# Spreading the experts' gates by transfers from DRAM instead of selector matmuls, with a ring for h

## The chip, the cores and the metric

One core of one Trainium2 chip. Times are device microseconds of one execution; the time of the kernel before is the median of three runs. The profile is of one execution of the same kernel.

## The reference, cut to what matters

A block of cross attention is followed by a mixture of experts. With x (after attention and a residual) normalised to xf, 1024 tokens of 128 features, 64 experts of 64 hidden features, and the 8 best experts of each token:

```python
aff = xf @ centroids.T
_, idx = top_k(aff + expert_biases, 8)
w = sigmoid(take_along_axis(aff, idx)); w = w / (sum(w) + 1e-8)
cw = zeros((T, E)).at[arange(T)[:, None], idx].add(w)
h = silu(einsum('td,edf->etf', xf, W_up))
y = einsum('etf,efd->etd', h, W_down)
routed = einsum('etd,te->td', y, cw)
x = x + silu(xf @ Ws_up) @ Ws_down + routed
```

The kernel computes all 64 experts for all tokens and multiplies h by the gate cw, which is zero for the experts that a token did not choose.

## The kernel before, in words

The attention stage (to about 294 us) runs 32 steps of pair and batch; then x is normalised again, the gates are found, and the expert stage runs. Its work is tiled into 32 expert tiles f: two experts of 64 hidden features fill the 128 rows, and the 1024 tokens are the columns. Everything there is in transposed form, rows are hidden features.

For each tile, by engine:
- **TensorE** (from L866 on): `up(f)` is six fp32r matmuls of 512 columns, two halves of the tokens by three terms (high by high, high by low, low by high: `three`, L715 to L720, whose lines L718 to L720 carry up and down alike). `spread(f)` (L936 to L944) is two f16 matmuls that multiply a selector, a column cut of `sel16`, by `cwT16`, and leave in PSUM bank CW_BANK the gate of each row's expert for all tokens. `down(f)` (L949) is six matmuls that add into the Y banks. The loop at L989 does spread(f+2), up(f+6), down(f) for f from 0 to 15; the rest is an order written out by hand, `closing` (L197 to L206), with one spread ahead of every third half of up or down.
- **ScalarE**: `silu(f)` (L670) moves up's result from PSUM to `h`; `h_high(f)` (L675) rounds the weighted h into `h_hi`, a ring of two, once down(f-2) is done. They alternate: h_high(f), silu(f+5).
- **VectorE**: `weigh(f)` (L1336, instruction L1340) multiplies h in place by the spread gates in PSUM; `h_low(f)` (L1342, L1344) is h less h_hi. Order: weigh(f+2), h_low(f+1). The last six tiles have halves of their own, `last_hi` and `last_lo` (L1365), without a wait for down.
- **GpSimd**: `split_up(f+6)` and then `split_down(f)` (L431 to L439) cut 128 x 128 weights into a high and a low half, one cast (L425) and one subtraction (L428) each; the halves have two buffers, so split_up(f) waits for up(f-2) and split_down(f) for down(f-2). L462 to L466 do the same for the last six tiles.
- **SyncE** issues the transfers, in order (L286 to L342). It issues none in the expert stage but the output's.

`h` has room for all 32 tiles ([P, 32, 1024] in f32). Ahead of the stage, VectorE makes `combine`, the gates as tokens by experts, splits it into two f16 terms `cw16` (L1326 to L1332); TensorE transposes them in eight transposes behind up(3) (L958 to L967), VectorE copies the result to `cwT16` (L1334). The selector is built by GpSimd (`pick16`, L363 to L368, at the start of the kernel) and spread by ScalarE in two fills, `fill_selector` (L625 to L632 and L653), among the roots and normalisations of the second norm: fill 0 stands ahead of xh (L648), fill 1 ahead of `root2(3, 3)` (L654), which the second half of the expert input waits for.

The lines that set the order around the change:

```python
            with pe.Fori(0, CLOSING // 2) as i:
                for u in range(2):
                    f = i * 2 + u
                    spread(f + 2)
                    pe.wait_ge(s_silu, f + (LEAD - 1))
                    up(f + LEAD, u)
                    down(f, u)
```

Of the kernel before, what the change touches and what calls it, by code (L numbers as in the profile page):

```python
# [32 lines left out]
P = 128  # L33
# [9 lines left out]
def xattn_moe(nc, x, ctx_in, mask, g_x, b_x, g_l, b_l, wq, wkv, wout, g_o, b_o,  # L43
# [14 lines left out]
    LEAD = 6  # L58
    assert D == P and TILES == 4 and KEYS == 512 and NT == 8 and LEAD % 2 == 0

    stack = ExitStack()
    with stack:
# [4 lines left out]
        def lay(offset, specs):  # L67
# [12 lines left out]
        (ident, one16, ident16, zeros16, cols, stats, mv, rs, shift, tmp, pick16, ones, range_v, neg_max, p_bias, ln_range, p_sum, p_rinv,  # L80
         ), top = lay(base, [
            ("ident", [P, P], F32), ("one16", [P, P], F16), ("ident16", [P, P], F16), ("zeros16", [P, 512], F16),
            ("cols", [P, 4], F32), ("stats", [P, 2 * NT, 6], F32), ("mv", [P, 2 * NT, 2], F32),
            ("rs", [P, 2 * NT], F32), ("shift", [P, 2 * NT], F32), ("tmp", [P, 2, 2 * NT], F32),
            ("pick16", [P, E], F16), ("ones", [P, P], F32), ("range_v", [P, 8], F32),
# [16 lines left out]
        v_base = max(end1, end2)  # L102
# [32 lines left out]
        (h,), h_end = lay(h_base, [("h", [P, FT, T], F32)])  # L135
        over = -(-(h_end - raw_base) // (P * 4))
        assert over <= FT - LEAD and h_base + T * 4 <= v_end


        (outT,), _ = lay(h_base, [("outT", [P, T], F32)])  # L140
        (yT, y_out, last_hi, last_lo, last_wd_hi, last_wd_lo), last_end = lay(h_base, [
# [6 lines left out]
        UNDER = -(-(last_end - h_base) // (T * 4))  # L148
        assert UNDER + LEAD < LAST

        SCRATCH = 10
        (xh, xfT, hs, biased, left, gate, combine, cw16), end3 = lay(h_base + (FT - SCRATCH) * T * 4, [
            ("xh", [P, NT, P], F32), ("xfT", [P, T], F32), ("hs", [FF, T], F32),
            ("biased", [P, NT, E], F32), ("left", [P, NT, E], F32),
            ("gate", [P, NT, E], F32), ("combine", [P, NT, E], F32), ("cw16", [P, NT, 2, E], F16),
        ])
        assert SCRATCH <= FT - LEAD and end3 <= raw_base

        (sel16, h_hi, h_lo, cwT16, wd_hi, wd_lo, wu_hi, wu_lo, wsu_hi, wsu_lo, xf_hi, xf_lo), end3 = lay(step_base, [
            ("sel16", [P, E, FF], F16), ("h_hi", [P, 2, T], F32R), ("h_lo", [P, 2, T], F32R),  # L160
            ("cwT16", [P, T], F16), ("wd_hi", [P, 2, P], F32R), ("wd_lo", [P, 2, P], F32R),
# [100 lines left out]
        s_cw, s_cwt, s_cwT, s_sel = sem("s_cw"), sem("s_cwt"), sem("s_cwT"), sem("s_sel")  # L262
        s_pick = sem("s_pick")
# [4 lines left out]
        s_u, s_cwb, s_silu, s_h, s_hhi, s_hlo, s_down = (sem("s_u"), sem("s_cwb"), sem("s_silu"),  # L268
# [17 lines left out]
        def _(sp):  # L286
# [61 lines left out]
        def _(pool):  # L348

            pool.memset(ident[:, :], 0.0).then_inc(s_pool, 1)  # L350
            pool.memset(one16[:, :], 0.0).then_inc(s_pool, 1)
            pool.memset(ident16[:, :], 0.0).then_inc(s_pool, 1)
            pool.memset(zeros16[:, :], 0.0).then_inc(s_pool, 1)
            pool.memset(wkT[:, :, :, :], 0.0).then_inc(s_pool, 1)
            pool.memset(pick16[:, :], 0.0).then_inc(s_pick, 1)
            pool.memset(ones[:, :], 1.0).then_inc(s_pool, 1)
            pool.memset(ln_range[:, :], LN_RANGE16).then_inc(s_pool, 1)
            pool.wait_ge(s_pool, 3)
            for m, fill in ((ident, 1.0), (one16, 1.0), (ident16, 1.0 / RANGE16)):
                pool.affine_select(out=m[:, :], in_=m[:, :], compare_op=ALU.not_equal, fill=fill,  # L360
                                   base=0, pattern=[[-1, P]], channel_multiplier=1).then_inc(s_pool, 1)

            pool.wait_ge(s_pick, 1)  # L363
            for part in range(2):
                pool.affine_select(out=pick16[:, :], in_=pick16[:, :], compare_op=ALU.not_equal,
                                   fill=1.0 / RANGE16, base=-part * E, pattern=[[-1, E]],
                                   channel_multiplier=1).then_inc(s_pick, 1)
                pool.wait_ge(s_pick, part + 2)  # L368

# [100 lines left out]
        def _(act):  # L470
# [51 lines left out]
            act.wait_ge(s_pool, 10)  # L522
# [102 lines left out]
            def fill_selector(half):  # L625

                cut = slice(half * E // 2, (half + 1) * E // 2)
                act.activation(sel16[:, cut, :], pick16[:, cut].unsqueeze(2).broadcast_to([P, E // 2, FF]),  # L628
                               ACT.Copy).then_inc(s_sel, 1)

            act.wait_ge(s_pick, 3)
            fill_selector(0)  # L632

# [19 lines left out]
            fill_selector(1)  # L653
# [16 lines left out]
            def silu(f, u):  # L670
                act.wait_ge(s_u, f + 1)
                act.activation(h_all[:, bass.ds(f * T, T)].rearrange("p (a c) -> p a c", a=2),  # L672
                               ps[:, U_BANK + 2 * u:U_BANK + 2 * u + 2, :], ACT.Silu).then_inc(s_silu, 1)

            def h_high(f, u, guard=True):  # L675
                act.wait_ge(s_h, f + 1)
                if guard:
                    act.wait_ge(s_down, f - 1)
                act.activation(h_hi[:, u, :], h_all[:, bass.ds(f * T, T)], ACT.Copy).then_inc(s_hhi, 1)  # L679
# [15 lines left out]
            with act.Fori(1, LAST // 2 - 1) as i:  # L695
                h_high(i * 2 + 1, 1)
                silu(i * 2 + LEAD, 0)
                h_high(i * 2 + 2, 0)
                silu(i * 2 + (LEAD + 1), 1)
# [14 lines left out]
        def _(pe):  # L714
# [8 lines left out]
            pe.wait_ge(s_pool, 10)  # L723
# [212 lines left out]
            def spread(f, guard=True):  # L936

                if guard:
                    pe.wait_ge(s_h, f)
                w = sel16[:, :, :].rearrange("p e f -> p (e f)")[:, bass.ds(f * P, P)]  # L940
                for half in range(2):
                    mm = pe.matmul(ps[:, CW_BANK + half, :], w, cwT16[:, half * 512:(half + 1) * 512],  # L942
                                   start=True, stop=True)
                mm.then_inc(s_cwb, 1)  # L944

# [31 lines left out]
            spread(1)  # L977

# [53 lines left out]
        def _(dve):  # L1032
# [266 lines left out]
            def find(half):  # L1299
# [3 lines left out]
                for j in range(4 * half, 4 * half + 4):  # L1303
# [18 lines left out]
            chain(dve.tensor_scalar(w_sum[:, 0, :], w_sum[:, 0, :], COMBINE_EPS, 1.0 / RANGE16, ALU.add, ALU.mult))  # L1322
# [3 lines left out]
            chain(dve.tensor_tensor(combine[:, :, :], gate[:, :, :],  # L1326
                                    w_sum[:, 1, :].unsqueeze(2).broadcast_to([P, NT, E]), ALU.mult))
            chained()
            chain(dve.tensor_copy(cw16[:, :, 0, :], combine[:, :, :]))
            chained()  # L1330
            dve.tensor_tensor(cw16[:, :, 1, :], combine[:, :, :], cw16[:, :, 0, :], ALU.subtract)\
               .then_inc(s_cw, 1)  # L1332
            dve.wait_ge(s_cwt, 1)
            dve.tensor_copy(cwT16[:, :], ps[:, CW_BANK, :].bitcast(F16)).then_inc(s_cwT, 1)  # L1334

            def weigh(f):  # L1336
                dve.wait_ge(s_silu, f + 1)
                dve.wait_ge(s_cwb, f + 1)
                hv = h_all[:, bass.ds(f * T, T)].rearrange("p (a c) -> p a c", a=2)
                dve.tensor_tensor(hv, hv, ps[:, CW_BANK:CW_BANK + 2, :], ALU.mult).then_inc(s_h, 1)  # L1340

            def h_low(f, u):  # L1342
                dve.wait_ge(s_hhi, f + 1)
                dve.tensor_tensor(h_lo[:, u, :], h_all[:, bass.ds(f * T, T)], h_hi[:, u, :].bitcast(F32), ALU.subtract)\  # L1344
# [9 lines left out]
            with dve.Fori(0, CLOSING // 2) as i:  # L1354
                for u in range(2):
                    weigh(i * 2 + (2 + u))
                    h_low(i * 2 + (1 + u), 1 - u)
            for what, f in closing_low:
# [41 lines left out]
```

## Time and profile before

| what | before |
|---|---|
| median of three runs | 431.31 us (430.63 to 432.95) |
| the profiled execution: its time, which is its span | 431.2 us |
| TensorE busy | 359.6 us (83%) |
| VectorE busy | 278.3 us (65%) |
| ScalarE busy | 280.7 us (65%) |
| GpSimd busy | 272.8 us (63%) |
| expert stage | about 322 to 425 us |

Busy times of the engines are sums over the whole span, and stages with different limits are mixed in them; the rows below are of the expert stage and of what leads to it. In rows of a timeline the first number is the start in us, the second the duration in us, then engine, line, operation, what it writes and what it reads; in square brackets is the idle time of the engine before it and what ended that. PE is TensorE, DVE VectorE, ACT ScalarE, POOL GpSimd, SPq SyncE's queue. Under the name L425 or L428 stand the casts and subtractions for up's and down's weights alike. A matmul's recorded duration is longer than the step from one to the next, since they are pipelined.

### The profile page before, as it was taken

Reading aid. Unit: us, or ns where it says so; the run is one execution under the profiler, and the core shown is the slowest. Engines: PE = TensorE matmul, PEld = TensorE weight load, DVE = VectorE, ACT = ScalarE, POOL = GpSimd, SP = SyncE. Lnnn points to the kernel's source line nnn. Section 1 sums busy time; section 2 is a strip of 40 time slices with the busy share of each in tenths; the row PEclk is TensorE's granted clock in tenths of the full one; section 3 lists DMA queues with packets and bytes.
Section 4 is the critical chain, followed back from the end, with each engine's and each line's share of the span. In section 5 each row is a group of like instructions: output and inputs, shape, how many; then the busy total and the mean of one; then the engine's idle time right before and its main releaser. Section 6 shows DMA issues by size and latency. Waiting matters only on the chain. (4 is left out here: it accounts for less than half of the span.)

```text
span 431.2 us, 7500 instructions
## 1 busy us (share of the span) xinstructions
PE 359.6 (83%) x2225; PEld 273.1 (63%) x2225; DVE 278.3 (65%) x668; ACT 280.7 (65%) x571; POOL 272.8 (63%) x347
## 2 busy tenths in 40 slices
PE   3669789888979999889798897843489999999996
PEld 2447557666757777667676676633266777777774
DVE  2889677646564657465665555505767877777795
ACT  3777786858585687775876767630558666666671
POOL 4222045878678798877987877752314677776682
PEclk9999989999998999999999998986559999999999
DMA  7200053998997989999989899991000000000001
GB/s 237 68 0 2 0 97 58 179 172 164 167 156 147 186 164 174 177 168 174 173 148 196 151 163 181 145 215 51 0 1 1 2 0 0 0 0 0 2 0 49
DMA packets 154913, 42.76 MB, mean 99 GB/s; under 512 B 144768, under 2 KB 154496, under 8 KB 154880
## 3 DMA queue, kind: packets, MB, share of 16 engines
q1 hardware_dynamic: 154448, 40.78, 52.1%
q10 hardware_dynamic: 432, 1.57, 1.1%
q8 instruction: 16, 0.26, 0.3%
q14 instruction: 17, 0.14, 0.1%
HBM read 8.26 MB, written 0.52 MB: 20 GB/s over the span
## 5 line engine op out<-in xcount | busy, mean ns | idle before, releaser
L396 POOL TENSOR_TENSOR p<-prob,p 128x512 f16<-128x512 f32 x128 | 145.9, 1166 | 48.2 <-ACT p L567 47.2
L1160 DVE CUSTOM_DVE_ANT_0 sc<-ps,mask_add 128x512 f32<-128x512 f32 x128 | 87.8, 691 | 46.3 <-PE ps L720 25.2
L551 ACT ACTIVATE prob<-sc,p_bias 128x512 f32<-128x512 f32 x128 | 90.6, 710 | 0.1
L816 PE MATMUL ps<-pT,v 128*64 128x256 f16 x768 | 53.0, 291 | 33.0 <-DMA pT<-p 33.0
L567 ACT ACTIVATE p<-prob 128x512 f16<-128x512 f32 x64 | 40.3, 630 | 49.2 <-DMA pT<-p 48.4
L816 PEld LDWEIGHTS ps<-pT,v 128*64 128x64 f16 x768 | 44.8, 117 | 39.1 <-issue 39.0
L388 POOL CAST p<-prob 128x512 f16<-128x512 f32 x64 | 39.0, 614 | 20.7 <-DMA pT<-p 20.4
L1340 DVE TENSOR_TENSOR h<-h,ps 128x1024 f32<-128x1024 f32 (+1 forms) x32 | 39.1, 1221 | 18.6 <-PE ps L942 17.3
L718 PE MATMUL ps<-kv_hi,q_hi 128*128 128x512 f32 x128 | 50.8, 397 | 0.0
L720 PE MATMUL ps<-kv_hi,q_lo 128*128 128x512 f32 x128 | 50.0, 390 | 0.0
L719 PE MATMUL ps<-kv_lo,q_hi 128*128 128x512 f32 x128 | 49.9, 390 | 0.0
L1180 DVE TENSOR_TENSOR ao<-ps,rinv_sb 128x256 f32<-128x256 f32 x32 | 13.6, 425 | 47.7 <-PE ps L839 47.5
L672 ACT ACTIVATE h<-ps 128x1024 f32 (+1 forms) x32 | 32.7, 1027 | 17.1 <-PE ps L720 17.1
L425 POOL CAST wu_hi<-wup_s 128x128 fp32r (+1 forms) x30 | 24.6, 819 | 24.5 <-PE ps L720 24.3
L679 ACT ACTIVATE h_hi<-h 128x1024 fp32r (+1 forms) x26 | 27.6, 1061 | 13.1 <-PE ps L720 12.0
L1344 DVE TENSOR_TENSOR h_lo<-h,h_hi 128x1024 fp32r<-128x1024 f32 x26 | 32.2, 1239 | 0.0
L559 ACT ACTIVATE p_bias<-neg_max,ln_range 128x2 f32<-128x2 f32 x64 | 18.2, 285 | 18.7 <-DVE neg_max L1160 18.7
L839 PE MATMUL ps<-ao,wo_s 128*128 128x256 f32 x64 | 24.0, 459 | 6.7 <-DVE ao L1180 6.7
L718 PE MATMUL ps<-xf_hi,wu_hi 128*128 128x512 f32 x60 | 28.8, 480 | 0.0
L1194 DVE SCALAR_TENSOR_TENSOR v<-ps,range_v,v 128x512 f16<-128x512 f32 x32 | 23.1, 749 | 7.2 <-ACT v L580 7.1
L718 PEld LDWEIGHTS ps<-kv_hi,q_hi 128*128 128x128 f32 x128 | 24.0, 188 | 5.6 <-DVE neg_max L1160 0.4
L720 PEld LDWEIGHTS ps<-kv_hi,q_lo 128*128 128x128 f32 x128 | 24.0, 188 | 5.3
(194 smaller groups left out, 745.0 us busy)
## 6 DMA issues: line engine op xcount, KB each, us to landing
pT<-p SPq DMA_TRANSPOSE x128, 3.3
wup_s<-in_L_ffn_W_up SPq DMA_DIRECT2D x8, 256.0 KB, 3.6
wdn_s<-in_L_ffn_W_down SPq DMA_DIRECT2D x8, 256.0 KB, 4.6
wkv_s<-in_L_xattn_Wkv ACTq DMA_DIRECT2D x2, 512.0 KB, 6.9
x_in<-in_x SPq DMA_DIRECT2D x2, 256.0 KB, 8.0
wq_s<-in_L_xattn_Wq ACTq DMA_DIRECT2D x1, 512.0 KB, 7.6
tok<-in_ctx SPq DMA_DIRECT2D x4, 128.0 KB, 8.1
wo_s<-in_L_xattn_Wout SPq DMA_DIRECT2D x1, 512.0 KB, 5.4
```

The costliest lines, as they stand in the source:

```text
L388: pool.tensor_copy(p16[:, t, 0, :], prob[:, t, :]).then_inc(s_phi_pool, 1)
L396: pool.tensor_tensor(p16[:, t, 1, :], prob[:, t, :], p16[:, t, 0, :], ALU.subtract).then_inc(s_plo, 1)
L551: act.activation(prob[:, t, :], sc[:, t, :], ACT.Exp, bias=p_bias[:, t:t + 1], scale=-1.0, accum_out=p_sum[:, i % 2, t:t + 1]).then_inc(s_ ...
L567: act.activation(p16[:, t, 0, :], prob[:, t, :], ACT.Copy).then_inc(s_phi_act, 1)
L672: act.activation(h_all[:, bass.ds(f * T, T)].rearrange("p (a c) -> p a c", a=2), ps[:, U_BANK + 2 * u:U_BANK + 2 * u + 2, :], ACT.Silu).th ...
L718: pe.matmul(o, a_hi, b_hi, start=start, stop=False, skip_group_check=skip)
L719: pe.matmul(o, a_hi, b_lo, start=False, stop=False, skip_group_check=skip)
L720: return pe.matmul(o, a_lo, b_hi, start=False, stop=stop, skip_group_check=skip)
L816: mm = pe.matmul(ps[cut, AV_BANK, 0:S], v16[:, b * KT + j, v, pair * P + head * DH:pair * P + (head + 1) * DH], pT[:, i % 2, head, p * KT ...
L1160: return dve.tensor_tensor_reduce(sc[:, t, :], ps[:, SCORE_BANK + (i * TILES + t) % SCORE_BANKS, :], mask_add[:, i % B, :], -SCALE, -LEAST ...
L1340: dve.tensor_tensor(hv, hv, ps[:, CW_BANK:CW_BANK + 2, :], ALU.mult).then_inc(s_h, 1)
L1344: dve.tensor_tensor(h_lo[:, u, :], h_all[:, bass.ds(f * T, T)], h_hi[:, u, :].bitcast(F32), ALU.subtract)\
```

## The change

The selector, its two f16 terms and the selector matmuls go. The gates are made in f32 (`combine`, laid out as four tiles of two token halves by 64 experts), turned by four f32 transposes, copied to `cwT` (rows: token half by expert; 512 columns) and stored to a DRAM buffer `kept` of 256 KB. For each tile SyncE then issues two transfers, one for each expert, that read that expert's two rows of 512 gates and write them into all 64 rows of the tile in `spread_w`, a ring of four slots; the transfers of tile f wait until weigh(f-4) is done. `weigh` reads `spread_w`. `h` has 12 slots: silu(f) waits for h_low(f-12). What shared its memory (scratch, last_hi and so on) moves behind the ring, so that the wait of the first `last_hi` for old tiles goes. ScalarE's and VectorE's loops are written out. The order of the remaining matmuls and of `closing_low` is the same.

```diff
...
+        (spread_w, cwT, h_hi, h_lo, wd_hi, wd_lo, wu_hi, wu_lo, wsu_hi, wsu_lo, xf_hi, xf_lo), end3 = lay(step_base, [
+            ("spread_w", [P, SLOTS, T], F32), ("cwT", [P, T // 2], F32), ("h_hi", [P, 2, T], F32R), ("h_lo", [P, 2, T], F32R),
...
+        kept = nc.dram_tensor("gates_turned", [P, T // 2], F32, kind="Internal").ap()
...
+            sp.wait_ge(s_cwT, 1)
+            sp.dma_start(kept, cwT[:, :]).then_inc(s_kept, 16)
+            sp.wait_ge(s_kept, 16)
+            for f in range(FT):
+                if f >= SLOTS:
+                    sp.wait_ge(s_h, f - SLOTS + 1)
+                for part in range(2):
+                    e = 2 * f + part
+                    sp.dma_start(spread_w[part * FF:(part + 1) * FF, f % SLOTS, :].rearrange("p (a t) -> p a t", a=2),
+                                 kept.rearrange("(a e) t -> e a t", a=2)[e:e + 1, :, :].broadcast_to([FF, 2, T // 2]))\
+                        .then_inc(s_gates[f % SLOTS], 16)
...
-            act.wait_ge(s_pick, 3)
-            fill_selector(0)
-
...
-            fill_selector(1)
             root2(3, 3)
...
             def silu(f, u):
                 act.wait_ge(s_u, f + 1)
-                act.activation(h_all[:, bass.ds(f * T, T)].rearrange("p (a c) -> p a c", a=2),
+                if f >= RING:
+                    act.wait_ge(s_hlo, f - RING + 1)
+                act.activation(h[:, f % RING, :].rearrange("p (a c) -> p a c", a=2),
                                ps[:, U_BANK + 2 * u:U_BANK + 2 * u + 2, :], ACT.Silu).then_inc(s_silu, 1)
...
-                    for j in range(NT):
-                        mm = pe.transpose(t16[:, j * P:(j + 1) * P],
-                                          cw16[:, j, :, :].rearrange("p a e -> p (a e)"), one16[:, :])
+                    for j in range(NT // 2):
+                        mm = pe.transpose(ps[:, CW_BANK, j * P:(j + 1) * P],
+                                          combine[:, j, :, :].rearrange("p a e -> p (a e)"), ident[:, :])
                     mm.then_inc(s_cwt, 1)
-                if f == LEAD - 1:
-                    pe.wait_ge(s_sel, 2)
-                    pe.wait_ge(s_cwT, 1)
-                    spread(0, guard=False)
...
-            spread(1)
-
...
-                    spread(f + 2)
                     pe.wait_ge(s_silu, f + (LEAD - 1))
                     up(f + LEAD, u)
                     down(f, u)
-            for what, f, half in closing:
+            for what, f, half in halves:
...
             def weigh(f):
                 dve.wait_ge(s_silu, f + 1)
-                dve.wait_ge(s_cwb, f + 1)
-                hv = h_all[:, bass.ds(f * T, T)].rearrange("p (a c) -> p a c", a=2)
-                dve.tensor_tensor(hv, hv, ps[:, CW_BANK:CW_BANK + 2, :], ALU.mult).then_inc(s_h, 1)
+                dve.wait_ge(s_gates[f % SLOTS], 32 * (f // SLOTS + 1))
+                dve.tensor_tensor(h[:, f % RING, :], h[:, f % RING, :], spread_w[:, f % SLOTS, :], ALU.mult).then_inc(s_h, 1)
...
```

## Rows read from the trace of the kernel before

**Rows 1.** Windows: stretch, its us, busy us of PE, PEld, DVE, ACT, POOL, PEclk, DMA

```profile
340.00:380.00 40.00, 40.00 (x178) 29.99 (x177) 30.00 (x26) 26.23 (x26) 29.26 (x52) 1.00 0.00 0
```

**Rows 2.** The chain of work that ended last: start us, us, engine and line, merged

```profile
342.63 0.45 PE ps L942 x2
...
345.81 0.45 PE ps L942 x2
```

**Rows 3.** Timeline of GpSimd and VectorE over one expert tile, 354 to 358 us

```profile
353.99 1.22 DVE L1344 TENSOR_TENSOR h_lo<-h,h_hi 128x1024 fp32r<-128x1024 f32 x1
...
354.17 1.18 POOL L425 CAST wu_hi<-wup_s 128x128 fp32r x1 [0.48 <-PE ps L720]
...
355.53 0.46 POOL L428 TENSOR_TENSOR wu_lo<-wup_s,wu_hi 128x128 fp32r<-128x128 f32 x1 [0.18 <-POOL wu_hi L425]
...
355.94 0.29 POOL L425 CAST wd_hi<-wdn_s 128x128 fp32r x1
...
356.02 1.22 DVE L1340 TENSOR_TENSOR h<-h,ps 128x1024 f32 x1 [0.82 <-PE ps L942]
...
356.41 0.47 POOL L428 TENSOR_TENSOR wd_lo<-wdn_s,wd_hi 128x128 fp32r<-128x128 f32 x1 [0.18 <-POOL wd_hi L425]
...
357.16 1.22 DVE L1344 TENSOR_TENSOR h_lo<-h,h_hi 128x1024 fp32r<-128x1024 f32 x1
```

**Rows 4.** Timeline of GpSimd and VectorE in the closing part, single rows

```profile
381.86 0.46 POOL L428 TENSOR_TENSOR wd_lo<-wdn_s,wd_hi 128x128 fp32r<-128x128 f32 x1 [0.18 <-POOL wd_hi L425]
...
393.27 1.44 POOL L428 TENSOR_TENSOR wu_lo<-wup_s,wu_hi 128x128 fp32r<-128x128 f32 x1 [0.18 <-POOL wu_hi L425]
...
412.22 0.47 POOL L428 TENSOR_TENSOR wd_lo<-wdn_s,wd_hi 128x128 fp32r<-128x128 f32 x1 [0.18 <-POOL wd_hi L425]
...
421.87 1.32 POOL L465 TENSOR_TENSOR last_wd_lo<-wdn_s,last_wd_hi 128x128 fp32r<-128x128 f32 x1
...
422.79 1.48 DVE L1365 TENSOR_TENSOR last_lo<-h,last_hi 128x1024 fp32r<-128x1024 f32 x1
```

**Rows 5.** Groups by line, VectorE, 335 to 384 us

```profile
L1340 DVE TENSOR_TENSOR h<-h,ps 128x1024 f32 x16 | 19.5, 1221 | 12.0 <-PE ps L942 12.0
```

**Rows 6.** Timeline of the hand-over, 306 to 314 us: ScalarE and VectorE

```profile
306.22 1.89 ACT L628 ACTIVATE sel<-pick 128x2048 f16<-128x2048 f16 x1
...
307.39 0.16 DVE L1279 SCALAR_TENSOR_TENSOR shift<-mv,rs 128x4 f32<-128x4 f32 x1
...
312.02 1.89 ACT L628 ACTIVATE sel<-pick 128x2048 f16<-128x2048 f16 x1
```

**Rows 7.** Timeline of the stage's opening, 327 to 337 us

```profile
327.53 0.69 DVE L1334 COPY cwT<-ps 128x1024 f16<-128x1024 f16 x1 [1.31 <-PE ps L965]
...
329.50 1.22 DVE L1340 TENSOR_TENSOR h<-h,ps 128x1024 f32<-128x1024 f32 x1
...
330.75 1.06 ACT L679 ACTIVATE h_hi<-h 128x1024 fp32r<-128x1024 f32 x1 [0.75 <-DVE h L1340]
...
334.74 0.39 PE L718 MATMUL ps<-h_hi,wd_hi 128*128 128x512 f32 x1
...
336.73 0.29 POOL L425 CAST wd_hi<-wdn_s 128x128 fp32r x1
```

**Rows 8.** DMA: issues with median us to landing; stretches 290.7 to 291.9, 13.0 to 14.4

```profile
wup_s<-in_L_ffn_W_up SPq DMA_DIRECT2D x8, 256.0 KB, 3.6
...
out<-y_out SPq DMA_DIRECT2D x2, 256.0 KB, 2.5
...
mask_u<-in_mask_BxS_bf SPq DMA_DIRECT2D x1, 128.0 KB, 4.8
...
DMA packets 802, 0.41 MB, mean 338 GB/s; under 512 B 9, under 2 KB 802, under 8 KB 802
...
DMA packets 262, 0.18 MB, mean 132 GB/s; under 512 B 25, under 2 KB 262, under 8 KB 262
```

**Rows 9.** The page's 40 slices: granted clock of TensorE in tenths

```profile
PEclk9999989999998999999999998986559999999999
```

More of the change, by code:

```diff
@@ L58, in xattn_moe @@
     LEAD = 6
+    SLOTS = 4
+    RING = 12
     assert D == P and TILES == 4 and KEYS == 512 and NT == 8 and LEAD % 2 == 0
@@ L78, in xattn_moe @@
         base = (nc.sbuf_base + 31) // 32 * 32
[L80 removed]
+        (ident, zeros16, cols, stats, mv, rs, shift, tmp, ones, range_v, neg_max, p_bias, ln_range, p_sum, p_rinv,
          ), top = lay(base, [
[L82 removed]
+            ("ident", [P, P], F32), ("zeros16", [P, 512], F16),
             ("cols", [P, 4], F32), ("stats", [P, 2 * NT, 6], F32), ("mv", [P, 2 * NT, 2], F32),
             ("rs", [P, 2 * NT], F32), ("shift", [P, 2 * NT], F32), ("tmp", [P, 2, 2 * NT], F32),
[L85 removed]
+            ("ones", [P, P], F32), ("range_v", [P, 8], F32),
             ("neg_max", [P, TILES], F32), ("p_bias", [P, TILES], F32), ("ln_range", [P, 1], F32), ("p_sum", [P, 2, TILES], F32),
@@ L132, in xattn_moe @@
         ])
-        (h,), h_end = lay(h_base, [("h", [P, FT, T], F32)])
-        over = -(-(h_end - raw_base) // (P * 4))
-        assert over <= FT - LEAD and h_base + T * 4 <= v_end
+        (h,), last_base = lay(h_base, [("h", [P, RING, T], F32)])
+        assert h_base + T * 4 <= v_end
         (outT,), _ = lay(h_base, [("outT", [P, T], F32)])
-        (yT, y_out, last_hi, last_lo, last_wd_hi, last_wd_lo), last_end = lay(h_base, [
+        (yT, y_out, last_hi, last_lo, last_wd_hi, last_wd_lo), last_end = lay(last_base, [
             ("yT", [P, T], F32), ("y_out", [P, NT, P], F32),
@@ L147, in xattn_moe @@
         LAST = FT - LEAD
[L148 to L152, printed above, removed]
+        assert last_end <= raw_base and RING > LEAD + 2
+        (xh, xfT, hs, biased, left, gate, combine), end3 = lay(last_base, [
             ("xh", [P, NT, P], F32), ("xfT", [P, T], F32), ("hs", [FF, T], F32),
             ("biased", [P, NT, E], F32), ("left", [P, NT, E], F32),
-            ("gate", [P, NT, E], F32), ("combine", [P, NT, E], F32), ("cw16", [P, NT, 2, E], F16),
+            ("gate", [P, NT, E], F32), ("combine", [P, NT // 2, 2, E], F32),
         ])
[L157 to L161, printed above, removed]
+        assert end3 <= raw_base
+        (spread_w, cwT, h_hi, h_lo, wd_hi, wd_lo, wu_hi, wu_lo, wsu_hi, wsu_lo, xf_hi, xf_lo), end3 = lay(step_base, [
+            ("spread_w", [P, SLOTS, T], F32), ("cwT", [P, T // 2], F32), ("h_hi", [P, 2, T], F32R), ("h_lo", [P, 2, T], F32R),
+            ("wd_hi", [P, 2, P], F32R), ("wd_lo", [P, 2, P], F32R),
             ("wu_hi", [P, 2, P], F32R), ("wu_lo", [P, 2, P], F32R),
@@ L261, in xattn_moe @@
         s_xres = sem("s_xres")
-        s_cw, s_cwt, s_cwT, s_sel = sem("s_cw"), sem("s_cwt"), sem("s_cwT"), sem("s_sel")
-        s_pick = sem("s_pick")
+        s_cw, s_cwt, s_cwT = sem("s_cw"), sem("s_cwt"), sem("s_cwT")
+        s_gates = [sem(f"s_gates{n}") for n in range(SLOTS)]
+        s_kept = sem("s_kept")
         s_sw, s_su, s_ssilu, s_shi, s_slo, s_sd = (sem("s_sw"), sem("s_su"), sem("s_ssilu"),
@@ L350, in _ @@
             pool.memset(ident[:, :], 0.0).then_inc(s_pool, 1)
-            pool.memset(one16[:, :], 0.0).then_inc(s_pool, 1)
-            pool.memset(ident16[:, :], 0.0).then_inc(s_pool, 1)
             pool.memset(zeros16[:, :], 0.0).then_inc(s_pool, 1)
             pool.memset(wkT[:, :, :, :], 0.0).then_inc(s_pool, 1)
-            pool.memset(pick16[:, :], 0.0).then_inc(s_pick, 1)
             pool.memset(ones[:, :], 1.0).then_inc(s_pool, 1)
             pool.memset(ln_range[:, :], LN_RANGE16).then_inc(s_pool, 1)
[L358 to L368, printed above, removed]
+            pool.wait_ge(s_pool, 1)
+            pool.affine_select(out=ident[:, :], in_=ident[:, :], compare_op=ALU.not_equal, fill=1.0,
+                               base=0, pattern=[[-1, P]], channel_multiplier=1).then_inc(s_pool, 1)
             pool.wait_ge(s_wvhi, 1)
@@ L694, in _ @@
             silu(LEAD + 1, 1)
[L695 to L699, printed above, removed]
+            for f in range(3, LAST - 1):
+                h_high(f, f % 2)
+                silu(f + LEAD - 1, (f + 1) % 2)
             h_high(LAST - 1, 1)
@@ L934, in _ @@
             up_half(1, 1).then_inc(s_u, 1)
[L936 to L944, printed above, removed]
             def down_half(half, w_hi, w_lo, h_hi, h_lo):
@@ L995, in _ @@
                     down(f, u)
-            for what, f, half in closing:
+            for what, f, half in halves:
                 cut = slice(half * 512, (half + 1) * 512)
-                if what == "spread":
-                    spread(f)
-                elif what == "up":
+                if what == "up":
                     if half == 0:
@@ L1321, in _ @@
             chained()
-            chain(dve.tensor_scalar(w_sum[:, 0, :], w_sum[:, 0, :], COMBINE_EPS, 1.0 / RANGE16, ALU.add, ALU.mult))
+            chain(dve.tensor_scalar(w_sum[:, 0, :], w_sum[:, 0, :], COMBINE_EPS, None, ALU.add))
             chained()
@@ L1353, in _ @@
             h_low(0, 0)
[L1354 to L1357, printed above, removed]
+            for f in range(CLOSING):
+                weigh(f + 2)
+                h_low(f + 1, (f + 1) % 2)
             for what, f in closing_low:
```

37 lines of the change are left out of this document (13 added, 24 removed).

## The prediction, made before the changed kernel was run

> **What bounds the kernel now.** I read the page first, then the table of windows, the chain that ended last, the timeline of one expert tile, the groups by line, and last the DMA view. The change lies in the expert stage (322 to 425 us) and in the hand-over before it. From 340 to 380 us TensorE is busy in all of 40 us at a granted clock of 1.00, with VectorE at 30.0 and GpSimd at 29.3 of them [rows 1]. The chain agrees: it is TensorE alone, with a pair of selector matmuls of 0.45 us once a tile and 3.18 us from one pair to the next [rows 2]; the other twelve matmuls of a tile step 0.23 us apart, 2.75 us together. So TensorE sets the pace and the selector work is 0.45 of every 3.18 us. VectorE's weighing stands idle behind it (12.0 us over 16 tiles) [rows 5].
>
> The timeline of one tile shows who is next [rows 3]. GpSimd has four instructions a tile (two casts, two subtractions). They take 2.71 us from 354.17 to 356.88, after a wait of 0.48 us for TensorE. But the cast at 354.17 takes 1.18 us, while its twin at 355.94 takes 0.29. The first ran beside h_lo, a VectorE subtraction with both inputs in SBUF; the second began as the weighing did, whose second input is in PSUM, and neither it nor the subtraction of 0.47 us behind it was lengthened. The subtraction too is stretched when it meets a VectorE instruction with two SBUF inputs (1.44, 1.32 us), and such a VectorE instruction is stretched in turn (1.48 instead of 1.22 us) [rows 3, 4]. The two engines take turns.
>
> **The change, part by part.** *TensorE:* 64 selector matmuls leave, 32 x 0.45 = 14.4 us, all on the path today. Four f32 transposes replace eight f16 ones; I count no difference, both stand behind up(3) in TensorE's order.
>
> *The weighing:* it now reads h and spread_w, both in SBUF. Its own 1.22 us stays (h_lo of this very form takes 1.22). It becomes a second instruction per tile that GpSimd must stand aside for. Price: a blocked cast costs 1.18 - 0.29 = 0.89 us, a blocked subtraction 1.32 to 1.44 less 0.46, so 0.86 to 0.98 [rows 3, 4]. I take 0.89. GpSimd's step goes from 2.71 to 3.60 us; that eats its wait of 0.48 us and passes TensorE's new 2.75. Bounds: 3.42, when the 0.18 us that a subtraction waits for its cast absorbs part, and 4.18, below. So the pace goes from 3.18 to 3.60 us in spite of the matmuls saved: GpSimd is late next, through the weight halves that up and down wait for, and TensorE idles 0.85 us a tile.
>
> In the trace the blocked cast ends 0.14 us after h_lo, not a full 0.29, so part of an instruction hides under the other. The Trainium skill (SBUF — State Buffer, "Who interferes with whom") says that a VectorE instruction with two SBUF inputs and a GpSimd instruction that reads SBUF exclude each other for a whole instruction. The trace agrees on who meets whom (1.18 against 0.29 us) and less on the price. Taken to the letter, with no hiding, a step is 4 x about 0.44 + 2 x 1.22 = 4.18 us; by the rows it is 3.60. That ending is a rival below.
>
> *The head:* two fills of the selector leave ScalarE. The first ends at 308.1 and holds back xh, whose last input was ready at 307.55 (0.45 us saved, for a start is not quite an end); the second holds root2(3) back from 312.0 to 313.9 [rows 6]. Of that 1.9 us I count some 1.1, because TensorE's shared_up(0) stands ahead of the transposes that need its result. I take -1.5 us, bounds -0.4 and -2.4. The constants that GpSimd no longer makes lie before TensorE's first weights arrive: nothing. The two f16 copies that leave VectorE ended before TensorE reached its transposes: nothing.
>
> *New wait, gates through DRAM:* today cwT16 is copied by 328.22 and the first weighing starts at 329.50 [rows 7]. Then: 328.22 - 1.5 = 326.7; store of 256 KB 2.5 us (as out<-y_out); issue of the second half about 0.45, as SP's issues ahead of the stage; landing 3.6 us (as wup_s, 256 KB; bounds 2.5 and the 4.8 of the broadcast mask) [rows 8]. First weighing at 333.2. Behind it stand h_high(0) 1.06 on ScalarE, with silu(5) queued after it, and h_lo(0) behind weigh(1) on VectorE; so 333.2 + 1.22 + 1.06 + 0.1 + 1.2 = 336.8 for down(0), against 334.74 [rows 7]: +2.1 us. TensorE has nothing to do for some 5 us before it; should its clock fall to the 1.2 GHz level there, as it stands at 5 and 6 tenths in the hand-over where TensorE waits [rows 9], add 1 or 2 us. SP issues 64 transfers at some 0.5 us, 1 us a tile, with nothing but the output behind them: hidden. A tile's 512 KB at the 338 GB/s of x_res takes 1.6 us [rows 8], hidden behind 3.6 with a ring of four. The ring of h waits for an h_lo six tiles back: hidden. Unrolled loops: nothing.
>
> **The sum.** Today split_down(2) starts at 336.73 and split_down(25) ends at 412.69 [rows 4, 7]: 14 steps of 3.18, 9 of 3.37 in the closing part (from 382.32), and a rest of 0.9. After: split_down(2) waits for down(0), 336.8 + 1.4 = 338.2. Then 14 x 3.60, and 9 x 3.90 since the closing order has four weighings in three tiles (0.33 x 0.89 more), and 1.8 for the rest: 87.3 us, to 425.5; +12.8. The tail gives some back: the last six tiles' halves have buffers of their own, so VectorE, no longer waiting for TensorE's selectors, has h_lo(25) done by 421.4. Nine more instructions at 1.14 (the spacing of weigh and h_lo [rows 3]) plus 0.17 for a turn given to GpSimd (0.08 behind a cast, 0.26 in the 1.48 behind a subtraction) end near 433. GpSimd's twelve last instructions, from 425.5, get about six turns until then, the other six take 0.38 each, and they end at 435.4, where today the last low half ends at 424.27 [rows 4]: +11.1. What follows is unchanged. The profiled execution takes 431.2, the median is 431.31, so no correction: 431.2 + 11.1 = **442 us**, from 435 (step 3.42, no extra in the closing part) to 448 with the clock and the slower landing.
>
> **The rivals.**
> (1) *No turn-taking with the weighing, TensorE stays the bound: faster.* Place: GpSimd's step beside weigh. Price: 29 selector pairs after down(0), -13 us, against +2.1 at the opening, 431.2 - 11 = 420. It decides as soon as the step stays under 2.75 us, that is if a weighing costs GpSimd nothing. For it: today's weighing costs GpSimd nothing. Against it: it costs nothing with PSUM as a source, and h_lo of the new form costs 0.89.
> (2) *Half of it:* GpSimd's step near 3.2, the kernel ends within 0.5% of 431. It needs a price of about 0.5 us, under every row seen.
> (3) *Full exclusion:* 4.18 us a step. 23 x 4.18 + 9 x 0.33 x 1.22 + 2 = 102 us in place of 87: 15 later, 457. For it: h_lo's 1.48 us when it came second. Against it: the 0.14 us above.
> (4) *The gates' transfers become the pace.* A broadcast from one place in DRAM is in the trace as the mask's; the 1.4 us in which most of it moved show 132 GB/s [rows 8]. 0.524 MB a tile at that is 3.97 us; 333.2 + 31 x 3.97 = 456.3 for the last gate, 3.5 us of weighing and halves, 6.9 us to the end: 467. Against it: that stretch also ran out in it, packets of 1 KB or less.
> (5) *The change doesn't do what it says:* the spread leaves TensorE by the diff itself, so only the gain can be missing, which is my forecast.
>
> **How the numbers follow.** A measurement of this kernel can tell about 0.5%, 2.2 us, from no change. My case (435 to 448) gets 0.60, case 3 0.12, case 4 0.11, case 1 0.09, case 2 0.08. Slower than 433.5 us is 0.83, within 0.08, faster 0.09. The range runs from 431 to 460; it leaves out case 1 and most of case 4.
>
> **What would show it.** Right: in the tile timeline GpSimd's casts and subtractions at 1.0 to 1.4 us twice a tile, GpSimd without waits on TensorE, TensorE's idle time ended by wu or wd halves, 3.5 to 3.7 us a tile; the first weighing near 333, down(0) near 337. Wrong: GpSimd's instructions at 0.29 and 0.46 beside the weighing, or VectorE's idle time ended by spread_w's transfers, or a tile at 2.75 us.

## The result, and the profile after

The changed kernel takes 448.41 us (median of four runs, 447.00 to 449.15) where the kernel before takes 431.52 (four runs, 430.63 to 432.95): a ratio of 1.0387, 95% interval 1.0346 to 1.0427. It is slower by 16.9 us; the forecast was slower by 10.7, at 442.0 in a range of 431 to 460. The profiled execution took 449.15 us with a span of 447.3. The 431.2 us that the table of before gives as the profiled execution's time is its span alone: an execution takes some 1.7 to 2.1 us more than its span wherever both are on record.

The table of windows of the changed kernel, with the columns of [rows 1]:

```profile
335.00:340.00 5.00, 2.56 (x6) 2.08 (x7) 4.98 (x5) 2.88 (x4) 0.00 (x0) 0.50 1.06 230
340.00:380.00 40.00, 34.90 (x139) 25.18 (x139) 30.05 (x24) 24.03 (x23) 34.71 (x43) 0.99 0.69 173
```

From 340 to 380 us TensorE was busy in all of 40 us [rows 1]; now it is busy in 34.90, and GpSimd has risen from 29.26 to 34.71, although it ran 43 instructions there and not 52. An engine whose busy time rises while its count falls is running longer instructions. The last column is the transfers' 173 GB/s, new here.

The waits of the changed kernel from 342 to 420 us, summed by who waited for whom, say which work TensorE now misses:

```profile
PE ps L705 <- POOL wu_lo L427: 7.9, 14, 1.0
...
PE ps L705 <- POOL wd_lo L427: 4.3, 7, 1.1
```

Each row gives the wait in us, how often, and the longest. L705 is the first matmul of a product, and what it waits for are the low halves of up's and down's weights, GpSimd's work. The chain that ended last has turned over too. Its shares of the span by engine, before and then after:

```profile
PE 26%; ACT 2%; DVE 1%; issue 0%; DVEq 0%
...
POOL 11%; issue 8%; PE 6%; DVE 3%; DMA 2%; ACT 2%; POOLq 1%; SPq 0%; DVEq 0%
```

The timeline of GpSimd and VectorE over one expert tile, with one row of TensorE, the counterpart of [rows 3]:

```profile
357.60 0.46 POOL L427 TENSOR_TENSOR wd_lo<-wdn_s,wd_hi 128x128 fp32r<-128x128 f32 x1 [0.19 <-POOL wd_hi L424]
357.79 1.35 DVE L1307 TENSOR_TENSOR h_lo<-h,h_hi 128x1024 fp32r<-128x1024 f32 x1 [0.53 <-ACT h_hi L670]
358.00 1.28 POOL L424 CAST wu_hi<-wup_s 128x128 fp32r x1
...
359.06 1.30 DVE L1303 TENSOR_TENSOR h<-h,spread_w 128x1024 f32<-128x1024 f32 x1
...
359.47 1.22 POOL L427 TENSOR_TENSOR wu_lo<-wup_s,wu_hi 128x128 fp32r<-128x128 f32 x1 [0.18 <-POOL wu_hi L424]
360.63 0.29 POOL L424 CAST wd_hi<-wdn_s 128x128 fp32r x1
...
360.74 0.50 PE L705 MATMUL ps<-xf_hi,wu_hi 128*128 128x512 f32 x1 [0.91 <-POOL wu_lo L427]
361.02 1.23 DVE L1307 TENSOR_TENSOR h_lo<-h,h_hi 128x1024 fp32r<-128x1024 f32 x1 [0.65 <-ACT h_hi L670]
361.10 1.46 POOL L427 TENSOR_TENSOR wd_lo<-wdn_s,wd_hi 128x128 fp32r<-128x128 f32 x1 [0.18 <-POOL wd_hi L424]
```

The cast at 358.00 is long beside h_lo, as before, and now the subtraction at 359.47 is long beside the weigh, which in [rows 3] left GpSimd alone. In this tile a third one, the subtraction at 361.10, meets the next h_lo; on average two are long: from 352 to 388 us 19 of 40 GpSimd instructions last over 0.9 us, 1.9 in four, where in the kernel before it is 11 of 46, about one in four. TensorE's 0.91 us of idle time ends with that subtraction. From the end of split_down(6) to that of split_down(16) (358.06 to 393.62 us) ten tiles take 3.56 us each.

VectorE hardly waits for the transfers. Its group of weighs from 335 to 384 us, against [rows 5]:

```profile
L1303 DVE TENSOR_TENSOR h<-h,spread_w 128x1024 f32<-128x1024 f32 x15 | 20.4, 1361 | 1.1 <-DMA spread_w<-gates_turned 1.1
```

The wait for the selector matmuls, 12.0 us, has become 1.1; the weigh itself went from 1.221 to 1.361 us, since it now gives turns to GpSimd.

The opening of the stage in the changed kernel, the counterpart of [rows 7]:

```profile
324.65 0.69 DVE L1298 COPY cwT<-ps 128x512 f32<-128x512 f32 x1 [2.06 <-PE ps L941]
...
325.37 0.34 SPq L339 DMA_DIRECT2D gates_turned<-cwT  x1
...
327.39 17.86 SPq L346 DMA_DIRECT2D spread_w<-gates_turned  x18
...
332.69 1.23 DVE L1303 TENSOR_TENSOR h<-h,spread_w 128x1024 f32<-128x1024 f32 x1 [6.22 <-DMA spread_w<-gates_turned]
...
335.02 1.23 DVE L1303 TENSOR_TENSOR h<-h,spread_w 128x1024 f32<-128x1024 f32 x1 [1.11 <-DMA spread_w<-gates_turned]
...
337.44 0.79 PE L705 MATMUL ps<-h_hi,wd_hi 128*128 128x512 f32 x1 [6.86 <-DVE h_lo L1307]
...
340.16 0.63 PE L705 MATMUL ps<-xf_hi,wu_hi 128*128 128x512 f32 x1
...
340.55 0.43 POOL L424 CAST wd_hi<-wdn_s 128x128 fp32r x1 [8.84 <-PE ps L707]
```

The gates take 7.35 us from the end of their copy (325.34) to the first weigh: 2.0 to be stored and 5.3 from the first issue. The second weigh waits again, for the second tile of the ring. TensorE idles 6.86 us. In the window 335 to 340 above, in which the pause ends, the granted clock is 0.50, the 1.2 GHz level, and the six matmuls of down(0) take 2.72 us (337.44 to 340.16) where six steps of 0.23 make 1.38. The transfers from the first issue to the first weigh:

```profile
327.39:332.69 5.30, 3.19 (x13) 2.03 (x12) 0.00 (x1) 0.00 (x0) 2.68 (x8) 1.00 0.68 163
```

163 GB/s over 5.30 us are 0.86 MB, and the first tile is 0.52 of them.

And the tail:

```profile
424.07 1.06 ACT L670 ACTIVATE h_hi<-h 128x1024 fp32r<-128x1024 f32 x1 [1.68 <-PE ps L707]
...
425.16 1.22 DVE L1307 TENSOR_TENSOR h_lo<-h,h_hi 128x1024 fp32r<-128x1024 f32 x1 [1.51 <-ACT h_hi L670]
...
427.13 0.47 POOL L427 TENSOR_TENSOR wd_lo<-wdn_s,wd_hi 128x128 fp32r<-128x128 f32 x1 [0.18 <-POOL wd_hi L424]
...
434.18 4.10 DVE L1327 TENSOR_TENSOR last_lo<-h,last_hi 128x1024 fp32r<-128x1024 f32 x3
...
439.28 0.46 POOL L464 TENSOR_TENSOR last_wd_lo<-wdn_s,last_wd_hi 128x128 fp32r<-128x128 f32 x1
```

The last low half of a weight ends at 439.74; before, it ended at 424.27.

### The profile page after: what moved, and what is told of

Its sections match the earlier page's. It is cut to its first block and busy times, and to the rows that moved or that the text cites. A ratio compares the mean times of both kernels' runs of the same rounds, so it can differ in the third digit from the quotient of the medians.

```text
span 447.3 us, 7239 instructions
## 1 busy us (share of the span) xinstructions
PE 354.0 (79%) x2157; PEld 266.8 (60%) x2157; DVE 283.3 (63%) x666; ACT 276.7 (62%) x569; POOL 295.0 (66%) x340
## 5 line engine op out<-in xcount | busy, mean ns | idle before, releaser
L705 PE MATMUL ps<-kv_hi,q_hi 128*128 128x512 f32 x128 | 50.8, 397 | 0.0
L1303 DVE TENSOR_TENSOR h<-h,spread_w 128x1024 f32<-128x1024 f32 x32 | 43.6, 1370 | 7.9 <-DMA spread_w<-gates_turned 7.3
L663 ACT ACTIVATE h<-ps 128x1024 f32<-128x1024 f32 x32 | 32.7, 1025 | 19.6 <-PE ps L707 19.6
L670 ACT ACTIVATE h_hi<-h 128x1024 fp32r<-128x1024 f32 x26 | 27.6, 1060 | 26.5 <-PE ps L707 17.9
L705 PE MATMUL ps<-xf_hi,wu_hi 128*128 128x512 f32 x60 | 26.1, 435 | 8.2 <-POOL wu_lo L427 7.9
L427 POOL TENSOR_TENSOR wu_lo<-wup_s,wu_hi 128x128 fp32r<-128x128 f32 x30 | 28.9, 963 | 5.4 <-POOL wu_hi L424 5.4
L705 PE MATMUL ps<-h_hi,wd_hi 128*128 128x512 f32 x52 | 21.7, 418 | 12.3 <-DVE h_lo L1307 6.9
```

The lines of the kernel that those rows point to most:

```text
L427: pool.tensor_tensor(lo, w[:, bass.ds(f * P, P)], hi.bitcast(F32), ALU.subtract)\
L705: pe.matmul(o, a_hi, b_hi, start=start, stop=False, skip_group_check=skip)
L1303: dve.tensor_tensor(h[:, f % RING, :], h[:, f % RING, :], spread_w[:, f % SLOTS, :], ALU.mult).then_inc(s_h, 1)
```

## The experiments

The theory: VectorE's weigh has a second SBUF input, so GpSimd gives a second turn in each tile and its four instructions become the pace. Rivals: the transfers of 512 KB a tile are the pace, or disturb the engines; or the late opening is what costs.

**1. The weigh reads PSUM, the transfers stay.** The changed kernel, with the weigh's second operand taken from the two banks that the selector matmuls had used.

```diff
-                dve.tensor_tensor(h[:, f % RING, :], h[:, f % RING, :], spread_w[:, f % SLOTS, :], ALU.mult).then_inc(s_h, 1)
+                hv = h[:, f % RING, :].rearrange("p (a c) -> p a c", a=2)
+                dve.tensor_tensor(hv, hv, ps[:, CW_BANK:CW_BANK + 2, :], ALU.mult).then_inc(s_h, 1)
```

> The kernel after the change, but the weighing multiplies h by PSUM bank 6 and 7 instead of spread_w; the gates are left out of the product, all transfers and their waits stay. Turn-taking theory (GpSimd's reads stand aside for VectorE instructions with two SBUF inputs): the weighing no longer costs GpSimd anything, its four instructions a tile go back to one stretched and three at 0.29 to 0.47 us, the pace of a tile falls from 3.6 to TensorE's 2.75 us, and the span by some 20 us, to about 427 us in time, under both kernels. Rival, the gates' transfers or their waits set the pace: nothing changes, 448 us. Rival, the opening alone is at fault: nothing changes either.

Measured: 427.08 us (425.25 to 430.18), ratio to the kernel before 0.9869 (0.9824 to 0.9915). GpSimd and VectorE over one tile:

```profile
360.21 1.15 POOL L424 CAST wu_hi<-wup_s 128x128 fp32r x1
361.13 1.21 DVE L1304 TENSOR_TENSOR h<-h,ps 128x1024 f32<-128x1024 f32 x1
361.54 0.46 POOL L427 TENSOR_TENSOR wu_lo<-wup_s,wu_hi 128x128 fp32r<-128x128 f32 x1 [0.18 <-POOL wu_hi L424]
361.94 0.29 POOL L424 CAST wd_hi<-wdn_s 128x128 fp32r x1
362.42 0.47 POOL L427 TENSOR_TENSOR wd_lo<-wdn_s,wd_hi 128x128 fp32r<-128x128 f32 x1 [0.19 <-POOL wd_hi L424]
```

One long instruction in a tile, 2.75 us from one tile to the next, and the transfers run as before at 202 GB/s from 345 to 380 us. One operand's place is worth 21.3 us (448.41 - 427.08), and the rivals of the transfers as the pace and of the late opening as the whole loss fall, since both were kept. (By the ratios to the kernel before it is 22 us; each run's interval is about 0.4% to either side, so differences of two runs' medians here are good to 2 or 3 us.)

**2. The weigh reads SBUF, no transfers.** The kernel before, its selector matmuls and waits kept, with another SBUF tensor as the weigh's second operand.

```diff
-                dve.tensor_tensor(hv, hv, ps[:, CW_BANK:CW_BANK + 2, :], ALU.mult).then_inc(s_h, 1)
+                dve.tensor_tensor(hv, hv, xf_hi[:, :].bitcast(F32).rearrange("p (a c) -> p a c", a=2), ALU.mult).then_inc(s_h, 1)
```

> The kernel before the change, with one edit: the weighing multiplies h by xf_hi in SBUF instead of by the spread gates in PSUM (the gates are left out of the product; the selector matmuls and the waits on them stay, and there are no transfers). Turn-taking theory: GpSimd's step goes from 2.7 us and a wait to about 3.6 us a tile without a wait, and the time from 431 to about 443 us. Rival, transfers or the round trip through DRAM are what costs: 431 us, no change.

Measured: 445.45 us (443.60 to 445.97), ratio 1.0313 (1.0278 to 1.0347). Two tiles of it:

```profile
347.63 1.23 DVE L1340 TENSOR_TENSOR h<-h,xf_hi 128x1024 f32 x1 [0.61 <-PE ps L942]
347.75 1.42 POOL L428 TENSOR_TENSOR wd_lo<-wdn_s,wd_hi 128x128 fp32r<-128x128 f32 x1 [0.18 <-POOL wd_hi L425]
...
351.62 1.38 DVE L1340 TENSOR_TENSOR h<-h,xf_hi 128x1024 f32 x1 [1.36 <-PE ps L942]
351.87 1.29 POOL L425 CAST wu_hi<-wup_s 128x128 fp32r x1
```

The subtraction of 0.46 and the cast of 0.29 are stretched beside the weigh, ten tiles from 344.25 to 380.18 us take 3.59 us each, and no transfer runs there. With the first run this settles the pace: the long step follows the operand, in both kernels, and needs nothing else of the change.

**3. No wait for the gates.** The changed kernel, its ring filled from rows of the weights of the output projection, which are in DRAM from the start.

```diff
-            sp.wait_ge(s_cwT, 1)
-            sp.dma_start(kept, cwT[:, :]).then_inc(s_kept, 16)
-            sp.wait_ge(s_kept, 16)
+            sp.wait_ge(s_wu, 2)
...
-                                 kept.rearrange("(a e) t -> e a t", a=2)[e:e + 1, :, :].broadcast_to([FF, 2, T // 2]))\
+                                 wout.rearrange("(n a k) d -> n a (k d)", a=2, k=4)[e:e + 1, :, :].broadcast_to([FF, 2, T // 2]))\
```

> The kernel after the change, but the ring of gates is filled from rows of an input in DRAM and needs no store of cwT, so its first four tiles are there before the first weighing (wrong gates, the same transfers otherwise). Turn-taking theory: the opening's wait goes (split_down(2) starts some 9 us earlier, near 331.7), the pace of 3.5 to 3.7 us a tile stays, time about 440 us. Rival, the round trip is the whole of the loss: 431 us or less. Rival, the opening is hidden under later waits: 448 us.

Measured: 446.45 us (443.51 to 446.85), ratio 1.0309 (1.0260 to 1.0358): 2.0 us under the changed kernel, little more than the noise of two such medians, so the expectation was missed by some 6 us. The opening shows where it went:

```profile
327.00 2.73 DVE L1301 TENSOR_TENSOR h<-h,spread_w 128x1024 f32<-128x1024 f32 x2
...
328.59 5.83 POOL L422 CAST wd_hi<-wdn_s 128x128 fp32r<-128x128 f32 x1
329.65 1.21 DVE L1305 TENSOR_TENSOR h_lo<-h,h_hi 128x1024 fp32r<-128x1024 f32 x1
330.79 1.21 DVE L1301 TENSOR_TENSOR h<-h,spread_w 128x1024 f32<-128x1024 f32 x1
331.92 1.21 DVE L1305 TENSOR_TENSOR h_lo<-h,h_hi 128x1024 fp32r<-128x1024 f32 x1
333.06 1.21 DVE L1301 TENSOR_TENSOR h<-h,spread_w 128x1024 f32<-128x1024 f32 x1
...
335.20 0.67 PE L703 MATMUL ps<-h_hi,wd_hi 128*128 128x512 f32 x1 [4.01 <-POOL wd_lo L425]
```

The first weigh starts at 327.00, but a cast of 0.29 us lasts 5.83: VectorE runs one two-input instruction behind the other, from 329.65 on none of them stretched, and no turn is given until they end. down(0) then waits for that weight until 335.20. The wait for the gates was gone and contention between the same instructions took its place. This run could not price the opening; the next one does.

**4. No wait for the gates and no contention by the weigh.** The edits of runs 1 and 3 together.

> e1 (the weigh reads the two idle PSUM banks, so that the gates are left out of the result) with the ring filled from rows of wout before the gates are there, as in e3: neither the weigh's second operand nor the wait for the store and the first landing is left. It prices the opening without the contention that hid it in e3. Theory (the first weigh 5.7 us late holds the first down product, and in e3 the saving was given back because VectorE's weighs kept GpSimd's cast off for 5.83 us): the weighs read one operand in SBUF here, no cast is held, the first weigh stands 5 to 6 us earlier and TensorE has no gap of 7 us: 427.1 less 5 to 8 = 419 to 422 us. Rival (the opening is hidden behind the weight splits in any case, and e3's 6 us over its forecast were the pace of the splits): within 1.5 us of e1, 426 to 428.5 us.

Measured: 416.23 us (414.34 to 417.85), ratio to a kernel before of 431.72 us 0.9636 (0.9595 to 0.9678). Its opening:

```profile
327.51 2.34 DVE L1302 TENSOR_TENSOR h<-h,ps 128x1024 f32<-128x1024 f32 x2
...
328.79 0.46 POOL L425 TENSOR_TENSOR wd_lo<-wdn_s,wd_hi 128x128 fp32r<-128x128 f32 x1 [0.18 <-POOL wd_hi L422]
...
331.57 0.39 PE L703 MATMUL ps<-h_hi,wd_hi 128*128 128x512 f32 x1
```

and the same product in run 1:

```profile
340.84 0.80 PE L705 MATMUL ps<-h_hi,wd_hi 128*128 128x512 f32 x1 [6.94 <-DVE h_lo L1308]
```

Without the weigh's contention the late gates cost 427.08 - 416.23 = 10.9 us (10 by the ratios), more than the 5 to 8 that I expected. Counted from the end of the first down weight's split, which stands before the wait (329.25 and 331.41), down(0) comes 7.1 us earlier (2.3 against 9.4 us behind it). The rest seems to lie in the work behind the pause: run 1's first matmuls are recorded at 0.80 us and not 0.39, and the granted clock is 0.61 from 335 to 340 us, where its TensorE is idle, and 0.50 from 340 to 345, where run 4 has 1.00 in both. How the remainder divides between the clock and the later landings was not tried.

**5. The whole result, with one operand of the weigh in PSUM.** From tile 6 on ScalarE's silu writes back to the banks that it read; the weigh multiplies those by the ring and writes h. The two idle banks are a third set for up, and VectorE's weighs run four tiles ahead of its subtractions, not two.

```diff
+        def tile_bank(f):
+            return (U_BANK, U_BANK + 2, CW_BANK)[f % 3] if f >= LEAD else U_BANK + 2 * (f % 2)
...
+                b = tile_bank(f)
+                o = ps[:, b:b + 2, :] if f >= LEAD else h[:, f, :].rearrange("p (a c) -> p a c", a=2)
+                act.activation(o, ps[:, b:b + 2, :], ACT.Silu).then_inc(s_silu, 1)
...
+                else:
+                    pe.wait_ge(s_h, f - 2)
...
+                dve.tensor_tensor(hv, ps[:, b:b + 2, :] if f >= LEAD else hv,
+                                  spread_w[:, f % SLOTS, :].rearrange("p (a c) -> p a c", a=2), ALU.mult).then_inc(s_h, 1)
```

> The changed kernel with the whole result computed, and with one operand of the weigh moved out of SBUF in another way: from tile 6 on ScalarE's silu writes its tile back to the PSUM banks that it read, and the weigh multiplies that by the ring of gates in SBUF and writes h. The two banks that the selector matmuls used are a third set for the up product, which waits for the weigh three tiles before; VectorE's weighs run four tiles ahead of its subtractions, not two. Tiles 0 to 5 as in the changed kernel. Theory (the step is longer because the weigh has two operands in SBUF, whatever they are): one stretched GpSimd instruction in a tile, a pace of 2.75 us from tile 7 on as in e1, the opening as in the changed kernel (split of tile 2 at about 340.5): e1's 427.1 and up to 2 us more for the six first weighs: 427 to 430 us, level with the kernel before or just under it. Rival (the transfers into the ring or the longer way from silu to weigh set the pace): 3.0 us or more in a tile, above 434 us.

Measured: 430.13 us (427.57 to 431.12), ratio to 431.72 us 0.9958 (0.9933 to 0.9982): just above the 427 to 430 of the theory, far from its rival's 434. A tile of it:

```profile
358.44 1.21 DVE L1313 TENSOR_TENSOR h<-ps,spread_w 128x1024 f32<-128x1024 f32 x1
358.85 0.46 POOL L429 TENSOR_TENSOR wu_lo<-wup_s,wu_hi 128x128 fp32r<-128x128 f32 x1 [0.18 <-POOL wu_hi L426]
359.26 0.29 POOL L426 CAST wd_hi<-wdn_s 128x128 fp32r x1
359.73 0.46 POOL L429 TENSOR_TENSOR wd_lo<-wdn_s,wd_hi 128x128 fp32r<-128x128 f32 x1 [0.18 <-POOL wd_hi L426]
```

The weigh still reads the gates from SBUF, its other operand comes from PSUM, and GpSimd is left alone: what matters is that there are two SBUF inputs, not which. Sixteen tiles from 365.25 to 408.87 us take 2.73 us each.

**6. The opening by matmuls, the rest by transfers.** Run 5, with the gates of tiles 0 and 1 spread by two float32 selector matmuls each; the ring starts at tile 2.

```diff
-            for f in range(FT):
-                if f >= SLOTS:
+            for f in range(FIRST, FT):
+                if f >= SLOTS + FIRST:
...
+            def spread(f):
+                for half in range(2):
+                    mm = pe.matmul(ps[:, CW_BANK + half, :], pick[:, f, half, :, :].rearrange("p a m -> p (a m)"), cwT[:, :],
+                                   start=True, stop=True)
+                mm.then_inc(s_cwb, 1)
...
+                if f < FIRST:
+                    dve.wait_ge(s_cwb, f + 1)
+                else:
+                    dve.wait_ge(s_gates[f % SLOTS], 32 * ((f - FIRST) // SLOTS + 1))
```

> e5 with the gates of tiles 0 and 1 alone spread by selector matmuls, as the kernel before does it, from the turned gates in float32 (two 128x512 matmuls a tile into the two banks that become the third up set); the ring of transfers starts at tile 2, and GpSimd builds the selector while it waits in the hand-over. The whole result is computed. Theory (in e5 the opening still costs what e4 against e1 priced at 10.9 us: the way through the store and the first landing puts weigh(0) at 334.4, TensorE has a gap of 7.3 us and its next matmuls are granted 0.66): weigh(0) at 329 to 330.5 us, down(0) at 334.5 to 336 in place of 339.7, tile 2's landing at about 334.5 is no longer first in line, the gap of TensorE is under 4 us, pace 2.75 us after it: 423 to 426 us, ratio 0.98 to 0.987. Rival (as in e3, the weighs of the opening hold GpSimd's splits back, so that an earlier start is lost again): 428.5 us or more, level with e5.

Measured: 426.15 us (423.28 to 430.85) against 432.39, ratio 0.9853 (0.9799 to 0.9907): clearly faster than the changed kernel, and than the kernel before by 0.9 to 2.0%; it ends just above the 423 to 426 us that were expected. Its opening:

```profile
328.00 0.69 DVE L1324 COPY cwT<-ps 128x512 f32<-128x512 f32 x1 [2.87 <-PE ps L963]
...
331.18 1.22 DVE L1334 TENSOR_TENSOR h<-h,ps 128x1024 f32<-128x1024 f32 x1 [1.37 <-PE ps L953]
...
336.82 1.22 DVE L1334 TENSOR_TENSOR h<-h,spread_w 128x1024 f32<-128x1024 f32 x1
```

The first weigh comes 2.5 us behind the copy of the gates and not 7.35; down(0) comes at 337.44, later than expected by 1.5 us, as is the copy itself in this execution (328.69 at its end, where run 5 has 327.19). The weigh of tile 2 finds its gates there, TensorE is busy in all of 325 to 340 us, and its granted clock stays at 1.00. Tiles 2 to 5 are still weighed with two SBUF inputs; what that costs here was not tried.

## Why the prediction was right, and where it was too small

**The mechanism was the forecast's.** The step of GpSimd was put at 2.71 + 0.89 = 3.60 us; it measured 3.56, and runs 1 and 2 show that this is the place of one operand. TensorE waits for the weight halves as said, and the transfers are covered by the ring. In the closing part 3.78 us came where 3.90 was forecast. From the start of split_down(2) to the end of split_down(25) the sum gave 87.3 us and the trace 87.05 (340.55 to 427.60). That this comes so close is in part luck: the first fourteen steps took 52.1 us where the sum had 50.4, for it is 3.56 only from tile 6 on and the tiles ahead of it took longer; the nine steps of the closing part took 34.0 where it had 35.1, and the last split 0.9 where it had 1.8. The rivals of no turn-taking (1), half of it (2), full exclusion (3) and transfers as the pace (4) are out: the steps that they need are 2.75, about 3.2, 4.18 and 3.97. For rival 4 the row that I used was the wrong neighbour: the mask's broadcast ran at 132 GB/s, this one moves 230 in the opening (last column of the window above), 2.3 us a tile. Rival 1 as a kernel is run 1, with the wait and without the weigh's contention: 427.08 us, not the rival's 420, for the wait cost 10.9 us there and not the 2.1 that it was priced at. Its price for the matmuls holds better: 420 less the 2.1 is 418, and run 4, without the wait, is at 416.

By the Trainium skill (SBUF — State Buffer, "Who interferes with whom") a VectorE instruction with at most one SBUF input (outside two-port modes, which the page says a tensor_tensor does not have) does not contend with GpSimd, and one with two contends with a GpSimd instruction that reads SBUF. The weighs of runs 1, 2 and 5 agree in both directions, with 0.46 us beside one and 1.42 beside the other. The Trainium skill (SBUF — State Buffer, "SBUF: two separate sides") adds that the one that waits is blocked for the whole instruction of the other. Taken as the prediction took it, with no hiding, that made a step of 4.18 us; the 3.56 do not bear that out as a price.

**The head** came out near the forecast in this pair of executions: from the shift's end to the copy's end 20.67 us before [rows 6, 7] and 18.95 after, so -1.7 where -1.5 was forecast. The other traces show how far that can be relied on: 20.32 in run 2, which has the old head, and 20.20, 19.26, 19.41 and 19.29 in runs 1, 3, 4 and 5, which have the new one. The saving lies between 0.1 and 1.7 us, about 1 on average, inside the bounds of 0.4 to 2.4 but for one trace. The shift itself ended 1.2 us earlier than in the execution of before, which is no part of the change: over the eight traces it ends anywhere between 304.8 and 308.4 us.

**Three terms were mis-sized.** The span came out at 447.3 where the sum said 442, 5.3 us more:

- *The opening, +2.35 us* (split_down(2) at 340.55, not 338.2; 3.5 if the shift had ended when it did before). The store took 2.0 us where 2.5 stood, but the first landing 5.3 where 0.45 + 3.6 stood. The step "landing 3.6 us (as wup_s)" priced the transfers of the first tile alone. SyncE issues eight for the four slots, one behind the other at 0.6 us, and 0.86 MB had moved by the first weigh where the first tile needs 0.52: it shared the engines with those behind it. How much of the 1.3 us that is was not tried. weigh(1) is held by the second tile of these, which the step did not have at all: "behind weigh(1)" took that weigh as ready. That brings down(0) to 337.44, 0.6 us later than the sum, although the copy was 1.4 us earlier than in it. The other 1.7 us lie between the start of down(0) and split_down(2), 3.1 us where the sum had 1.4: 1.3 of them are the clock (2.72 us for the six matmuls, not 1.38), for which the sum named 1 or 2 us and left them out, and 0.4 pass between the last of these matmuls and the cast, which the sum had at nothing.
- *The tail, +2.2 us.* "VectorE, no longer waiting for TensorE's selectors, has h_lo(25) done by 421.4" failed: it ended at 426.38. h_lo waits for h_hi, and that for the down product two tiles back, the very products that GpSimd's halves hold up (424.07 and 425.16 above, with 1.68 and 1.51 us of idle time before them). VectorE did not run ahead, so its last two-input instructions (eight of them, where the sum counted nine) came later, and GpSimd ended 12.1 us behind its last ring split (427.60 to 439.74) where the sum had 9.9.
- *The pace, -0.25, and the very end, +0.6.*

These are 4.9 together, and the sum's 442.3 had been rounded down to 442. They are read from one execution on either side, so a term is good to about 1 us, as the head shows. The other 1.1 us of the median's miss of 6.4 is what lies around the span: the profiled execution took 1.8 us more than its span (449.15 and 447.3), and "so no correction" took the span of before for the time.

**Where the expected gain is.** Taking the selector and its matmuls off the path, the two fills of the head included, is worth 15.5 us (431.72 to 416.23, run 4). The wait for the gates takes 10.9 of it (run 1), and the contention 21.3 more (448.41 against run 1). The two overlap: with the contention in place, taking the wait away gives 2.0 us (run 3), hardly clear of noise.

## What to carry to other kernels

Moving an operand from PSUM to SBUF can cost an engine that is not in the diff: before a VectorE instruction gets its second SBUF input, look at what GpSimd does beside an instruction of that form in the same trace, and price every such meeting in the step. Where data has to go through DRAM, let the first tiles take a short way and the transfers start behind them, and price the first landing with all the transfers that are issued beside it. A chain's tail is bound by the same late engine as its middle, unless every wait in it has been followed back.

## What had not been expected of the hardware

Turns between VectorE and GpSimd are not certain. In the steady stage a GpSimd instruction gets its turn at the end of one VectorE instruction (a cast takes 1.2 to 1.3 us); in run 3 a cast took 5.83 us while the VectorE instructions beside it stayed at 1.21. What decides between the two is open: no run separates it.

In the changed kernel and in runs 1 and 5 TensorE's pause of about 7 us is followed by matmuls recorded at 0.63 to 0.80 us (0.39 otherwise) and windows with a granted clock of 0.50 to 0.66. In run 3 a pause of 4.01 us is followed by the same: 0.63 to 0.67 us, and 0.66 from 335 to 340 us. In run 6, with no such pause, the granted clock stays at 1.00 from 325 to 345 us. The pause costs more than its length.
